# An attention block and a routed feed-forward block on one core: the output projection computed with the weights held in the array

## The reference

```
x = x + layernorm(attention(layernorm(x)))
x = x + layernorm(ffn(layernorm(x)))

attention: q = h @ Wq (16 heads of 64), k, v = h @ Wk, h @ Wv (4 heads of 64), rotary on q and k,
           causal softmax(q k / 8) v, heads side by side (1024 columns), @ Wo (1024 x 128)
ffn:       linear, swiglu, mixture of 8 experts (4 taken per token) with a shared one, linear, swiglu
```

## Time and profile before

| | |
|---|---|
| median of 3 runs | 1238.08 us (1237.53 to 1239.38) |
| profiled execution | 1239.26 us, of it span 1237.4 us |
| mean granted clock of TensorE | 0.971 |
| busy: PE, weight loads, DVE, ACT, POOL | 90%, 63%, 76%, 64%, 54% |
| instructions | 27070 |

### The profile page before, as it was taken

How to read it: one execution, slowest core, us unless ns; L and a number is a source line. 1 busy time by engine, 2 the same in 40 slices (tenths; PEclk the granted TensorE clock), 3 DMA queues, 4 the chain that set the end, 5 groups by cost and what they waited for, 6 DMA issues and landing times.

```text
span 1237.4 us, 27070 instructions
## 1 busy us (share of the span) xinstructions
PE 1108.4 (90%) x8712; PEld 774.4 (63%) x8712; DVE 935.3 (76%) x1862; ACT 789.5 (64%) x1741; POOL 668.6 (54%) x716
## 2 busy tenths in 40 slices
PE   3799999989999997899999879999987989999996
PEld 2566666676666665766666567666664856566563
DVE  6888888847888897588888965888886466666665
ACT  3577887737787875387787655787775344444444
POOL 1375776816775774375776633776753123333332
PEclk8799999989999998999999989999998999999999
DMA  6568778754878766278788463788675111221220
GB/s 172 135 154 204 186 181 208 189 141 105 201 159 203 182 150 153 62 158 204 183 181 195 103 151 94 186 183 197 153 178 115 70 69 69 78 77 78 78 78 26
DMA packets 138813, 175.94 MB, mean 142 GB/s; under 512 B 45296, under 2 KB 133488, under 8 KB 137584
## 3 DMA queue, kind: packets, MB, share of 16 engines
q1 hardware_dynamic: 137536, 174.57, 56.8%
q10 hardware_dynamic: 1200, 0.39, 0.1%
HBM read 24.06 MB, written 2.23 MB: 21 GB/s over the span
## 4 chain that ended last, share of the span: by engine, by line
PE 53%; DVE 20%; issue 13%; ACT 11%; DMA 1%; POOL 1%; DVEq 0%; SPq 0%; ACTq 0%; POOLq 0%
PE rows L495 12%; DVE neg_max L1201 8%; PE o_out L540 6%; ACT work L784 6%; PE proj_bank L437 3%; PE small L495 3%; PE o_out L693 3%; DVE work L1224 3%; ACT probsT L793 3%; PE rows L437 2%; PE o_out L454 2%; PE rows L438 2%; PE rows L439 2%; PE proj_bank L454 2%; PE proj_bank L439 2%
## 5 line engine op out<-in xcount | busy, mean ns | idle before, releaser
L1201 DVE TENSOR_REDUCE neg_max<-rows 128x1 f32<-128x1024 f32 (+3 forms) x256 | 248.9, 1013 | 126.8 <-PE rows L498 126.1
L784 ACT ACTIVATE work<-rows,neg_max 128x1024 f32<-128x1024 f32 (+3 forms) x256 | 242.7, 952 | 140.2 <-DVE neg_max L1201 138.2
L1224 DVE STREAM_TRANSPOSE work<-work 128x896 f32<-128x896 f32 (+6 forms) x448 | 288.9, 682 | 3.0 <-ACT work L784 0.9
L540 PE MATMUL o_out<-probsT,v_g 128*64 128x128 f32 (+1 forms) x3328 | 280.2, 319 | 4.9 <-DMA probsT<-work 4.6
L540 PEld LDWEIGHTS o_out<-probsT,v_g 128*64 128x64 f32 x3328 | 203.0, 137 | 73.7 <-issue 22.3
L1044 POOL TENSOR_TENSOR attnT<-o_raw 128x256 f32 (+1 forms) x128 | 93.8, 733 | 128.2 <-ACT o_raw L800 126.8
L784 ACT ACTIVATE work<-small,neg_max 128x128 f32<-128x128 f32 (+3 forms) x256 | 133.1, 529 | 41.8 <-DVE neg_max L1209 41.7
L1012 POOL TENSOR_TENSOR turned<-turned,cf 128x512 f32<-128x512 f32 x92 | 100.6, 1093 | 77.3 <-DVE turned L1193 77.3
L1059 POOL TENSOR_TENSOR roped<-raw,cf 128x512 f32<-128x512 f32 x92 | 100.5, 1092 | 65.8 <-ACT raw L753 65.8
L495 PE MATMUL rows<-kk,qh 64*128 64x512 f32 (+2 forms) x512 | 107.7, 417 | 24.7 <-ACT probsT L793 14.0
L1068 POOL TENSOR_TENSOR roped<-roped,turned 128x512 f32<-128x512 f32 x92 | 118.9, 1292 | 13.6 <-POOL turned L1012 0.4
(11 more groups left out here) (193 smaller groups left out, 2286.2 us busy)
## 6 DMA issues: line engine op xcount, KB each, us to landing
probsT<-work SPq DMA_DIRECT2D x512, 224.0 KB, 4.1
kk<-kk SPq DMA_DIRECT2D x16, 512.0 KB, 4.6
kl<-kl SPq DMA_DIRECT2D x16, 512.0 KB, 5.6
v_g<-v_all SPq DMA_DIRECT2D x32, 256.0 KB, 3.9
probsT<-scratch SPq DMA_DIRECT2D x4, 2048.0 KB, 7.0
attnT<-scratch SPq DMA_DIRECT2D x4, 2048.0 KB, 7.0
slab_a<-w_qk SPq DMA_DIRECT2D x15, 256.0 KB, 4.1
xm<-in_x SPq DMA_DIRECT2D x4, 512.0 KB, 8.7
```

Source lines behind the costliest of these rows:

```text
L540: ins = mm(dst.rearrange("p (k c i) -> p k c i", c=QUADS, i=QUAD), v_g[p][:, t, :], x, start=t == 0, stop=t == big_w - 1)
L784: A(probs[s % 2][:, q * 128:q * 128 + width], (rows if big else turn_bank)[h][:, 0:width], ACT.Exp, bias=neg_max[:, s % 2, item:item + 1], ...
L1201: V.tensor_reduce(neg_max[:, s % 2, h:h + 1], rows[h][:, 0:big_w * 128], AX_X, ALU.max, negate=True).then_inc(max_ready, 1)
L1224: V.transpose(dst, src).then_inc(fold_done, 1)
```

## The change

A half now runs eight products of 512 columns: the 128 x 128 block `w_o[:, s, :]` is stationary, and the attention values of four tiles are streamed past it. The result has the 128 output features on the partitions and 512 tokens along the bank. ACT copies it to `attn_out` (`keep_products`), PE turns each of its four 128 x 128 blocks with a transpose into the same bank (`turn_out`), and ACT copies the turned result to `attn_out` (`keep_out`, as before). In the batches both halves are multiplied first, then both are turned; ACT has the two new copies ahead of the two old ones. Behind the last batch the order on ACT is: copy of product 0, table load, gate exponents, copy of product 1, results 0 and 1, gates.

```diff
--- before.py
+++ after.py
@@ -246,8 +246,8 @@
         proj_done, raw_kept, cos_done, sin_done, rope_sum, rope_high, rope_low = map(sem, (
             "proj_done", "raw_kept", "cos_done", "sin_done", "rope_sum", "rope_high", "rope_low"))
         swapped = sem("swapped")
-        wo_done, wo_kept, mid_done, x_ready, x2_turned, x2_kept = map(sem, (
-            "wo_done", "wo_kept", "mid_done", "x_ready", "x2_turned", "x2_kept"))
+        out_done, out_kept, wo_done, wo_kept, mid_done, x_ready, x2_turned, x2_kept = map(sem, (
+            "out_done", "out_kept", "wo_done", "wo_kept", "mid_done", "x_ready", "x2_turned", "x2_kept"))
         lin0_done, h_kept, swi1_done, a_kept, h1_kept = map(sem, ("lin0_done", "h_kept", "swi1_done", "a_kept", "h1_kept"))
         gate_done, gate_z, gate_exp, gate_parts, gate_turned, comb_kept = map(sem, (
             "gate_done", "gate_z", "gate_exp", "gate_parts", "gate_turned", "comb_kept"))
@@ -449,10 +449,16 @@
 
             def project_out(a, dst):
 
+                for s in range(NP):
+                    ins = mm(dst[:, :], w_o[:, s, :], attnT[:, s, 4 * a:4 * a + 4, :].rearrange("p t c -> p (t c)"),
+                             start=(s == 0), stop=(s == NP - 1))
+                ins.then_inc(out_done, 1)
+
+            def turn_out(b, a, dst):
+
+                pe.wait_ge(out_kept, 2 * b + a + 1)
                 for t in range(4 * a, 4 * a + 4):
-                    for s in range(NP):
-                        ins = mm(dst[:, t % 4 * 128:t % 4 * 128 + 128], attnT[:, s, t, :],
-                                 w_o[:, s, :], start=(s == 0), stop=(s == NP - 1))
+                    ins = nc.tensor.transpose(dst[:, t % 4 * 128:t % 4 * 128 + 128], attn_out[:, t, :], ident)
                 ins.then_inc(wo_done, 1)
 
             def project_first(k, dst):
@@ -568,6 +574,8 @@
                         pe.wait_ge(ffn_w_in, 16 * FFN_LOADS)
                     project_out(0, proj_bank)
                     project_out(1, o_out)
+                    turn_out(b - 1, 0, proj_bank)
+                    turn_out(b - 1, 1, o_out)
                     pe.wait_ge(wo_kept, 2 * b - 1)
                 if last and s == project_step(0):
                     pe.wait_ge(x_split, 2 * b + 4 if b + 1 < B else 1)
@@ -727,6 +735,8 @@
             project_out(0, o_bank[0])
             gate(0, block_max[2])
             project_out(1, o_bank[1])
+            turn_out(B - 1, 0, o_bank[0])
+            turn_out(B - 1, 1, o_bank[1])
             turn_gate(0, side[1])
             pe.wait_ge(wo_kept, 2 * B)
             pe.wait_ge(wx_split, UP_PARTS)
@@ -815,11 +825,16 @@
                     act.wait_ge(rope_sum, ROPES_B * B + ROPES_G)
                     A(x2T[a], src[:, :], ACT.Copy).then_inc(x2_kept, 1)
 
-            def keep_out(b, a, src):
-
-                act.wait_ge(wo_done, 2 * b + a + 1)
+            def keep_products(b, a, src):
+
+                act.wait_ge(out_done, 2 * b + a + 1)
                 if a == 0 and b:
                     act.wait_ge(mid_done, b)
+                A(attn_out[:, 4 * a:4 * a + 4, :].rearrange("p t d -> p (t d)"), src[:, :], ACT.Copy).then_inc(out_kept, 1)
+
+            def keep_out(b, a, src):
+
+                act.wait_ge(wo_done, 2 * b + a + 1)
                 A(attn_out[:, 4 * a:4 * a + 4, :].rearrange("p t d -> p (t d)"), src[:, :], ACT.Copy).then_inc(wo_kept, 1)
 
             def keep_values(b):
@@ -844,6 +859,8 @@
                 if depth > 1 and shared:
                     keep_outputs(b, *earlier(g, s, 2))
                 if first and s == 1 and b:
+                    keep_products(b - 1, 0, proj_bank)
+                    keep_products(b - 1, 1, o_out)
                     keep_out(b - 1, 0, proj_bank)
                     keep_out(b - 1, 1, o_out)
                 if last and b == B - 1 and s >= 3:
@@ -985,9 +1002,11 @@
             keep_h(0)
             keep_a(0)
             keep_h1(0)
-            keep_out(B - 1, 0, o_bank[0])
+            keep_products(B - 1, 0, o_bank[0])
             nc.scalar.preload_act_table_set("natural_log_exp_and_others")
             gate_exponents(0)
+            keep_products(B - 1, 1, o_bank[1])
+            keep_out(B - 1, 0, o_bank[0])
             keep_out(B - 1, 1, o_bank[1])
             keep_gates(0)
             for n in range(CHUNKS):
```

More of the change, by code:

```diff
@@ L816, in keep_tokens @@
                     A(x2T[a], src[:, :], ACT.Copy).then_inc(x2_kept, 1)
+            def keep_products(b, a, src):
+                act.wait_ge(out_done, 2 * b + a + 1)
+                if a == 0 and b:
+                    act.wait_ge(mid_done, b)
+                A(attn_out[:, 4 * a:4 * a + 4, :].rearrange("p t d -> p (t d)"), src[:, :], ACT.Copy).then_inc(out_kept, 1)
             def keep_out(b, a, src):
                 act.wait_ge(wo_done, 2 * b + a + 1)
-                if a == 0 and b:
-                    act.wait_ge(mid_done, b)
                 A(attn_out[:, 4 * a:4 * a + 4, :].rearrange("p t d -> p (t d)"), src[:, :], ACT.Copy).then_inc(wo_kept, 1)
```

## The result

The changed kernel takes 1249.57 us in the median (8 runs, 1246.71 to 1251.21), the kernel before 1240.24 (8 runs, 1237.53 to 1244.67). (The medians alone stand 9.3 us apart, the means 8.3: 1249.03 and 1240.73.) The profiled executions have spans of 1248.0 and 1237.4 us and mean granted clocks of 0.968 and 0.971.

The account below looks back on a forecast made before the run. PE, busy 90% of the span, was taken as the bound, with the projection on the path in four places. 3 x 0.81 + 0.83 = +3.3 us on the median 1238.08 gave 1241.4 us; range for 8 in 10: 1237.8 to 1245.

Parts of the forecast that it names:

- The halves: Each projection half: eight products of 512 columns at 0.86 us take 6.88 us, gaining 0.27 us a half.
- Rival 3: Inside each half: loads that now delay records would be 48 fewer, so not slower, down to 1200 us; chance 0.04.
- The tails: Behind each second half: transposes and another ACT copy delay scores by 1.35 us, the last projection's next chunk by 1.37.
- Each link: Behind the second half: ACT's product copy ends at P+0.64, PE's transposes at P+1.36, ACT's result copy at P+2.00.
- P: The moment when the second half of a projection ends on PE; later events are given in us after it.
- the reading with P+2.24: In batches, step 2's scores start 0.24 us after ACT's last copy, 2.24 us behind the second half; now 0.89.
- the one with 2.44: Scores start 2.44 us behind the second half, if 0.19 us behind the rope projection belong to the projection's end.
- The sum: Over four projections: 3 x 0.81 us in the batches plus 0.83 us behind the last, +3.3 us.
- the likeliest case: Whole kernel: the summed +3.3 us holds, 1241.4 us, own range 1240 to 1243; chance 0.66.
- rival 2: First halves of the projection keep their clock: 1238.1 us if both 1.63 us losses go, 1239.8 if one; chance 0.12.
- Rival 1: Clock falls behind the second half, up to 1.63 us each in one to four places: 1243 to 1248; chance 0.10.
- the signs listed: Trace checks: halves 6.9 us, scores at P+2.2 to 2.4, chunk at P+2.05, 8 more ACT copies, DVE wait 0.8 us longer.

## Why the prediction was wrong

- **The halves**: right. 8 x 0.86 = 6.88, measured 6.88. The loads of 0.19 us lay beside the stream, in the traces before and after (a record every 0.112 and every 0.43 us at full clock). Rival 3 is out.
- **The tails**: right. +1.34 us each (2.23 for 0.89; 2.03 for 0.69) where +1.35 and +1.37 were worked out. Each link came as written. The rope projection came behind the first result's copy, as written: the copy ends at 282.86 and the first record starts at 282.92, P+1.18 for P+1.3, under the last transposes. And the reading with P+2.24 held, not the one with 2.44.
- **The sum**: 3.1 us for 3.3. Up to here it is the likeliest case, and these 3.1 us of the slowdown came for the reason given.
- **The failed step** is the one under "Sum", where I wrote "I put it on the median of the runs": the summed difference was put on the median as if the rest of the kernel stayed. The one sentence on it stood in rival 2: nothing made fewer low stretches likelier than more, "and the runs before had their own mix". That was an assumption of a neutral mix, and it is false here: the changed kernel's mean clock is 0.9660 for 0.9706, in every one of its 8 runs below the mean of the kernel before. Delays of 2.0 to 4.8 us by three different means cost 7 to 9 us, and of the change's 7.6 us some 4 are of this kind. The median itself was also a poor base. It was that of three runs, 1238.08, and eight runs of the same kernel have 1240.24: of the 8.2 us between the forecast 1241.4 and the measured 1249.57, 2.2 are this.
- **Rival 1** had the right agent in the wrong place. In the trace the clock did not fall behind P (1.00 in the 4 us behind all four projections, transposes included), and the first halves were low in two of three batches before and in one of three after. It fell one and two groups later, at an idle time of 1.65 us that the earlier trace rows don't hold, because I looked for idle time only around the change. Its bound of 1.63 us a fall was somewhat above what was measured there (1.06 to 1.4).
- The range was too narrow upward. It took single falls at four places, where the places at risk are all the steps with idle time, step 0 of nearly every group.
- Of the signs listed, halves, copies, transposes and both tails came right; the 0.8 us of DVE's wait too (14.93 us with the first half at full clock, against 15.79 - 1.63 = 14.16 for the kernel before without its low clock). None of them could show where the rest was. The page's mean clock could: 0.971 to 0.968, and 0.9706 to 0.9660 over the runs.

What stays open is why a shift of 0.7 us a batch meets the clock badly in most runs, rather than in as many as before. One guess is that PE works on from the end of a low stretch, so that the later steps come to lie alike against the clock in each execution; no run here tests it. A delay was tried at one place and in three sizes only.

## What to carry to other kernels

An edit that moves the later work by less than a microsecond a batch can cost several, where PE has idle stretches behind which its clock falls in some executions and not in others. So list PE's idle stretches over the whole kernel, compare the mean granted clock of many runs, not the one profile, and give the range room for it. And to learn an edit's own price, compare both versions with the idle stretches filled: here 7.6 us became 2.5 to 4, and the filling itself gained 4.6 us by the medians and 6 by the ratios, more than the change cost with the stretches filled.

## What was not expected of the hardware

- The same idle time of 1.65 us, at the same granted 1.00, was followed by stretches at 1.2 GHz in the changed kernel's execution and at 2.4 GHz in that of the kernel before, with the same instructions around it; one stretch costs 1.06 to 1.4 us in such a step and 1.63 in the first half of the projection, where PE works without a break. The Trainium skill ("TensorE: Matmul & The Clock Gate", Part 1) says that the window by which PE is judged is free-running and does not start with the kernel. The two executions agree with that; no run here shows the window itself.
- Useless products made a kernel 6 us faster (ratio 0.9951), though PE was already the busiest engine at 90%.
- The kernel before spreads over 12 us (1237.07 to 1249.10) with its mean clock, so that three runs with a spread of 1.9 us were no measure of its scatter.
